# The loop over two iterations becomes one straight order of 80 attention jobs, and the first pair's last layers stand between the second pair's jobs

## The reference, cut to what matters

```python
# L0: modulated norm, self-attention with rotary embedding, gate, cross-attention, gate, MLP (gelu), gate
x = x + g_msa * self_out;  x = x + g_x * cross;  x = x + g_mlp * mlp_out
# L1: cross-attention on a normalised context
x = x_q + (out @ Wp + bp)
# L2: self-attention, gate, cross-attention, MLP (gelu), gate
x = x + h * gate_msa;  x = x + h;  x = x + h * gate_mlp
# L3: one-head attention on the context, a router over 3 experts (silu), a sigmoid gate
weights = softmax(scores);  routed = sum_e expert_out_e * router_probs_e
x = x + g * (routed @ out_w + out_b)
```

## Time and profile before

| | |
|---|---|
| time before, median of 3 runs | 987.18 us (987.16 to 987.22) |
| the profiled execution's own time | 980.62 us |
| its span | 978.7 us |
| PE busy | 780.3 us (80%) |
| DVE, ACT, POOL busy | 468.3, 325.2, 203.1 us |
| mean granted TensorE clock | 0.856 of full speed |

### The profile page before, as it was taken

How to read it: one execution, slowest core, us unless ns; L and a number is a source line. 1 busy time by engine, 2 the same in 40 slices (tenths; PEclk the granted TensorE clock), 3 DMA queues, 4 the chain that set the end, 5 groups by cost and what they waited for, 6 DMA issues and landing times.

```text
span 978.7 us, 22436 instructions
## 1 busy us (share of the span) xinstructions
PE 780.3 (80%) x9226; PEld 474.7 (49%) x9226; DVE 468.3 (48%) x1111; ACT 325.2 (33%) x544; POOL 203.1 (21%) x239
## 2 busy tenths in 40 slices
PE   5688888787788788868947888878878878887797
PEld 4244444545454455554633445454544445555447
DVE  3557544444455755332146566545344676343403
ACT  0123334233323333325421233352423233224362
POOL 1323221212123322010013233213022223111000
PEclk9799978858778987689979999996777899659899
DMA  8300000000000000000031000000000000000000
GB/s 299 109 1 13 13 1 2 2 1 2 2 2 2 2 2 2 1 0 1 1 109 50 2 3 1 2 1 1 2 1 2 1 2 2 1 2 1 1 0 23
DMA packets 5360, 16.26 MB, mean 17 GB/s; under 512 B 1577, under 2 KB 2612, under 8 KB 4360
## 3 DMA queue, kind: packets, MB, share of 16 engines
q1 hardware_dynamic: 4588, 10.72, 3.3%
q10 hardware_dynamic: 668, 4.05, 1.1%
HBM read 13.66 MB, written 1.09 MB: 15 GB/s over the span
## 4 chain that ended last, share of the span: by engine, by line
PE 65%; ACT 13%; DVE 11%; issue 8%; POOL 1%; DMA 1%; DVEq 0%; SPq 0%; ACTq 0%; POOLq 0%
PE avp L1006 15%; PE lin L889 12%; PE big L981 11%; PE lin L902 10%; ACT P L528 7%; ACT hT L515 4%; PE big L957 3%; DVE mhl L734 2%; PE big L989 2%; PE lin L911 2%; PE big L977 2%; DVE hid L758 2%; PE mtp L963 2%; PE big L974 1%; DVE xn L696 1%
## 5 line engine op out<-in xcount | busy, mean ns | idle before, releaser
L528 ACT ACTIVATE P<-big 77x1024 f32<-77x1024 f32 (+1 forms) x160 | 154.6, 1017 | 406.0 <-PE big L989 406.0
L734 DVE TENSOR_REDUCE mhl<-big 128x8 bf16<-128x616 f32 (+1 forms) x160 | 152.8, 964 | 108.2 <-PE big L957 105.3
L889 PE MATMUL lin<-hT,W 128*128 128x512 f32 x184 | 115.4, 734 | 39.5 <-ACT hT L515 37.0
L469 POOL TENSOR_TENSOR qm<-qT,hm 128x512 f32<-128x512 f32 x80 | 88.6, 1108 | 198.6 <-PE big L989 104.3
L981 PE MATMUL big<-qm,kT 32*77 32x512 f32 (+1 forms) x640 | 111.1, 770 | 0.0
L1006 PE MATMUL avp<-P,Vp 77*32 77x128 f32 (+1 forms) x2560 | 99.7, 304 | 4.0 <-ACT P L528 4.0
L1006 PE MATMUL avp<-P,onesp 77*32 77x128 f32 (+1 forms) x2560 | 101.4, 308 | 0.0
L436 POOL TENSOR_SCALAR rstd<-mv 128x4 f32<-128x4 f32 (+1 forms) x36 | 8.3, 230 | 433.0 <-DVE mv L687 432.8
L957 PE MATMUL big<-kbm,qb 32*128 32x308 bf16 (+1 forms) x320 | 57.4, 359 | 50.4 <-ACT P L528 50.2
L1006 PEld LDWEIGHTS avp<-P,Vp 77*32 77x32 f32 (+1 forms) x2560 | 73.8, 120 | 29.9 <-issue 19.4
L1006 PEld LDWEIGHTS avp<-P,onesp 77*32 77x32 f32 (+1 forms) x2560 | 85.7, 126 | 1.2
(11 more groups left out here) (153 smaller groups left out, 843.2 us busy)
## 6 DMA issues: line engine op xcount, KB each, us to landing
gbc<-gate_rows SPq DMA_DIRECT2D x4, 1280.0 KB, 8.8
W<-in_w ACTq DMA_DIRECT2D x2, 1152.0 KB, 12.3
hid<-in_ws SPq DMA_DIRECT2D x2, 832.0 KB, 5.7
W<-in_w ACTq DMA_DIRECT2D x1, 1088.0 KB, 6.7
xin<-in_x SPq DMA_DIRECT2D x4, 256.0 KB, 4.8
out<-x SPq DMA_DIRECT2D x4, 256.0 KB, 2.2
ctx<-in_ctx SPq DMA_DIRECT2D x4, 154.0 KB
ctxT<-in_ctxT SPq DMA_DIRECT2D x4, 154.0 KB
```

Of the source, the lines that this page charges most:

```text
L469: nc.gpsimd.tensor_tensor(qm[:, j % 2], q.broadcast_to([128, 4, T]), mask.broadcast_to([128, 4, T]), ALU.mult).then_inc(qm_ready, 1)
L528: nc.scalar.activation(P[j % 2][0:kw, 8 * half:8 * half + 8, :], big[0:kw, 2 * half:2 * half + 2, :].rearrange("p g (h q) -> p (g h) q", h=4),
L734: v.tensor_reduce(mhl[:].rearrange("p (g c) -> p g c", c=32)[:, 2 * half:2 * half + 2, 0:4], big[:, 2 * half:2 * half + 2, 0:4 * kw].rearr ...
L889: i = mm(lin_ap(st, s, job, m)[:, 0:n], w, a, start=(c == 0), stop=(c == len(parts) - 1))
```

## The change

The loop goes. All 16 samples are held at once: `NS` is 4 groups, and `ORDER` lists 20 blocks of four jobs: groups 0 and 1 through all five attentions, then groups 2 and 3. There are 80 jobs in one list. Each group has seven chains of units (`CHAINS`), one ahead of each attention and one behind the last, and each unit has a share of the way from the chain's first slot to its last; a slot is a quarter of a job. For the last chain `TAILS` gives the slots: group 0's from job 36 to the start of job 51, group 1's from job 40 to the start of job 56; groups 2 and 3 run over the end.

So that this fits, `x` is loaded once into `xs` for all groups; the gates come one at a time through a ring of four (`gring`) in place of 1,280 KB for each group and iteration; `Vp` and `hid` are shared by groups 0 and 2 and by 1 and 3; there is one `P`; the rope and the gated sums use `oT` for their partial result. Norm semaphores are one per group. The waits are on constants.

```diff
-NS = 2
-ITERS = B // (GB * NS)
+NS = B // GB
...
-for _k in range(NAT):
-    UNITS += merge(_k, 0, BETWEEN[_k], 1) + merge(_k, 1, BETWEEN[_k + 1], 0)
-UNITS += [("END", None, None)] + weave([("B", u, 0) for u in LAST],
-                                       [("B", u, 1) for u in [u for _, u in BETWEEN[NAT]] + LAST])
+ORDER = [(k, 2 * pair + s) for pair in range(2) for k in range(NAT) for s in range(2)]
...
+TAILS = [(16 * 9, 16 * 12 + 12), (16 * 10, 16 * 14), (16 * 19, END + 60), (END, END + 60)]
...
+def chain_slots(k, s):
+
+    if k == NAT:
+        return TAILS[s]
+    end = 16 * POS[k, s] - 6
+    if k:
+        return 16 * (POS[k - 1, s] + 1), end
+    return max(16 * POS[k, s] - 28, 0), end
...
+            for share, u in chain:
+                slot = first + round(share * (last - first))
...
+for _slot in range(END):
+    UNITS.append(("A", _slot // 4, _slot % 4))
+    UNITS += [("B", u, s) for slot, u, s in PLACED if slot == _slot]
+UNITS += [("END", None, None)] + [("B", u, s) for slot, u, s in PLACED if slot >= END]
...
-        P = [sb(f"P{i}", [128, H, T]) for i in range(2)]
+        P = sb("P", [128, H, T])
...
+        Vp2 = [sb(f"Vp{i}", [128, GB, H, 32]) for i in range(2)]
+        hid2 = [sb(f"hid{i}", [128, 7, N]) for i in range(2)]
...
+            def values(a, s):
                 st, kw = f"p{a}", ATT[a]["kw"]
-                lin_ready(dve, it, st, s, "v")
+                earlier = [p for (_, s2), p in POS.items() if s2 % 2 == s % 2 and p < POS[a, s]]
+                if earlier:
+                    dve.wait_ge(av_full, job_turn(max(earlier) * GB + GB - 1))
+                lin_ready(dve, st, s, "v")
...
-            with pe.Fori(0, ITERS) as it:
-                for kind, u, s in UNITS:
+            for kind, u, s in UNITS:
```

More of the change, by code:

```diff
@@ L110 @@
[L110 to L121, removed]
-]
@@ L124 @@
[L124 to L131, removed]
-    out = []
[L134 to L137, removed]
@@ new lines, with values_slot, placed @@
+TAILS = [(16 * 9, 16 * 12 + 12), (16 * 10, 16 * 14), (16 * 19, END + 60), (END, END + 60)]
[6 more added lines that the diff above has]
+    return max(16 * POS[k, s] - 28, 0), end
+def values_slot(k, s):
+    p = POS[k, s]
+    before = [q for (_, s2), q in POS.items() if s2 % 2 == s % 2 and q < p]
+    return 16 * (max(before) + 1) if before else 0
+def placed():
+    out = []
+    for s in range(NS):
+        for k, chain in enumerate(CHAINS):
+            if (k, s) == (0, 0):
+                continue
+            first, last = chain_slots(k, s)
+            for share, u in chain:
+                slot = first + round(share * (last - first))
+                if u == (f"p{k}", "v"):
+                    slot = max(slot, values_slot(k, s))
+                    assert slot < 16 * POS[k, s] + 3
+                out.append((slot, u, s))
+    return sorted(out, key=lambda e: e[0])
@@ L164 @@
             _n += 1
-LIN_JOBS = _n
-assert LIN_JOBS % 2 == 0
 def lin_bank(st, s, job):
     return LIN_AT[(st, s, job)] % 2
[L173 to L181, removed]
@@ L183, with lin_turn @@
-GATED = ["o0", "o1", "m0", "o3", "m1", "x3"]
[L184 to L197, removed]
-def job_of(j):
-    return j // (NS * GB), j // GB % NS, j % GB
-def nth(it, k, s, kinds, b=0, per=1):
-    return it * (kinds * NS * per) + (k * NS + s) * per + b + 1
+def lin_turn(st, s, job):
+    return LIN_AT[(st, s, job)] // 2 + 1
@@ new lines, in order_of, with groups_of @@
+def order_of(s, *wanted):
+    return [u[0] for kind, u, s2 in UNITS if kind == "B" and s2 == s and u in wanted]
+def groups_of(unit):
+    return [s for kind, u, s in UNITS if kind == "B" and u == unit]
+GATED = ["o0", "o1", "m0", "o3", "m1", "x3"]
+LN_ORDER = [[int(st[1:]) for st in order_of(s, *((f"l{k}", "stat") for k in range(NLN)))] for s in range(NS)]
+GATED_ORDER = [order_of(s, *((st, "y") for st in GATED)) for s in range(NS)]
+GATE_USES = [(u[0], s) for kind, u, s in UNITS if kind == "B" and u[1] == "y" and u[0] in GATED and u[0] != "x3"]
@@ new lines, with norm_turn, gated_turn, job_turn @@
+QB_ORDER = [(int(u[0][1:]), s) for kind, u, s in UNITS if kind == "B" and u[0][0] == "p" and u[1] == "q"]
+NGB = 4
+assert all(groups_of(("x3", part)) == groups_of(("x3", "s")) for part in X3_PARTS)
+assert all(groups_of(("p0", part)) == list(range(NS)) for part in "kq")
+def norm_turn(k, s):
+    return LN_ORDER[s].index(k) + 1
+def gated_turn(st, s):
+    return GATED_ORDER[s].index(st) + 1
+def job_turn(j, part=0, per=1):
+    return j * per + part + 1
+def job_of(j):
+    return ORDER[j // GB] + (j % GB,)
@@ new lines, in _ @@
+            sp.wait_ge(gate_rows_out, 16)
+            for n in range(NGB):
+                gates(n)
+            used = 0
+            for kind, u, s in UNITS:
+                if kind == "B" and u[1] == "y" and u[0] in GATED:
+                    sp.wait_ge(x_ready[s], gated_turn(u[0], s))
+                    if u[0] == "x3":
+                        sp.dma_start(out[:, s * GB:(s + 1) * GB, :], xs[s][:]).then_inc(stored[s], 16)
+                    else:
+                        used += 1
+                        if used + NGB <= len(GATE_USES):
+                            gates(used + NGB - 1)
@@ L423, in _ @@
+            for s in range(NS):
+                sp.wait_ge(stored[s], 16)
         @block.gpsimd
@@ new lines, in _ @@
+            for kind, u, s in UNITS:
+                if kind == "START":
+                    act.wait_ge(gate_rows_out, 16)
+                elif kind == "A" and s == 0:
+                    exps(u, 0)
+                    exps(u, 1)
+                elif kind == "B":
+                    st, part = u
+                    k = int(st[1:])
+                    if part == "t":
+                        norm(k, s)
+                    elif st[0] == "p":
+                        project(k, s, part)
+                    elif st[0] == "m" and part != "y":
+                        mlp(k, s, int(part[1:]))
+                    elif st == "x3":
+                        mixture(s, part)
```

625 lines of the change are left out of this document (292 added, 333 removed), and 6 rows, old and new, of the table CHAINS.

## The result

The changed kernel takes **941.86 us** (median of 4 runs, 940.23 to 946.37), the kernel before took 987.20 beside it (987.16 to 996.67). The ratio is 0.9525, 95% interval 0.9459 to 0.9592. I had forecast 910 with a range of 885 to 945: the direction and the range held, and the size was off by 32 us, 45 us saved where 77 were forecast.

A forecast was written before the change was run, and what follows sets the result against it. PE was taken to bound the kernel, busy 780.3 of 978.7 us, with waits and a lowered clock. Terms −122.9 + 85 − 14 − 9 + 5 − 1 − 12 − 6 − 3 = −78 took 987.2 to 909, stated as 910, range 885 to 945.

The forecast's parts named there:

- The gap: Between the two iterations' attention jobs, 404.1 to 527.0 us: this stretch goes, −122.9 us.
- its PE work: PE work from the stretch between the iterations comes back between attention jobs: +85 us, +93 if nothing runs faster.
- the filled waits: In the 20 jobs receiving the moved work, units fill idle PE time: −14 us, bounds 0 and −29.
- the clock there: In the 20 jobs receiving the moved work, PE falls less to its lower clock: −9 us, between 0 and −14.
- the loads: On ACT, 18 more function table loads, 23.1 us, mostly hidden: +5 us, bounds 0 and +23.1.
- Rival B: ACT binds the mixed jobs, so all table loads show and the filling is lost: 942 us, chance 0.17.
- case A: The likeliest case, PE-bound filling as the terms sum: 885 to 932 us, chance 0.62.
- Rival C: The PE clock comes back everywhere, wider spacing lifting 0.83 and 0.77 to 0.93: 876 us, chance 0.15.
- Chains are spaced wider: In the chains, wider spacing of producers and consumers cuts PE's waits for `hT` and `xn`: −12 us, bounds 0 and −30.
- clock from fewer long waits: In the stretches at clock 0.83 and 0.77, fewer long waits make it fall less often: −6 us, bounds 0 and −79.
- Head (−1) and last tail (−3): Group 1's norm and keys leave the start, −1 us; `l7` and half of `m1`'s group 2 matmuls precede the end, −3.
- At nothing: Single `P`, the gate ring's loads and the wait for `av_full` ahead of `v` were each taken to cost nothing.

The follow-up runs named there:

- the one chain mended: The changed kernel with the whole chain between attentions 1 and 2 put back at the old kernel's quarters: 910.5 us, and 907.11 us when repeated.
- The block kernel: The changed kernel with the last layers of the first pair in one block at job 40 instead of between the second pair's jobs: 979.64 us.
- all chains set back: The changed kernel with all four chains between attentions at the old kernel's quarters, last layers and head still spread: 939.71 us.

## Why the forecast was right in direction and too large

*The gap, its PE work, the filled waits, the clock there, the loads (−56 together).* Right. The stretch saved 45.5 us as it was and 52.7 with the one chain mended (298.4 to 245.7), at the forecast clock of 0.95 to 0.96. The block kernel shows that 31 of the 45.5 us of the stretch are the laying between jobs. The terms give 223 us of busy PE and 20 of idle there; measured were 227.4 and 25.4, and with the chain mended 224.5 and 21.2. The load term of +5 was measured at about +6. The mark of 240 us was missed by 6 with the chain mended, by 13 without.

*Rival B, ACT binds the mixed jobs.* Not what happened. In the changed kernel PE's waits for `P` in that stretch are some 4 us, not over 30:

```profile
PE big L1001 <- DVE mT L751: 7.5, 4, 2.8
PE lin L923 <- DVE xn L702: 3.8, 1, 3.8
PE big L962 <- ACT P L546: 3.0, 5, 1.1
```

The time, 942, is where B had put it, by another cause. That it lies within the range is luck in part: case A alone ended at 932, and the range went to 945 for B's sake. The Trainium skill's rule (ScalarE: Activation LUTs, "Table sets: the hidden batching unit") would have the loads gathered; the run without them says that here this could bring at most some 8 us. Nor is the 2.66 us per switch of the Trainium skill (the same page, "What ACT_TABLE_LOAD costs") seen: 1.31 us lie between the end of the exponentials and the start of the gelu in job 13 (163.45 and 164.76), and the stretch fell by 7.9 us without 25 loads, where 25 times 2.66 would be 67.

*Rival C.* Not seen: the clock outside the mixed jobs was 0.77 to 0.82 in jobs 12 to 36 and 56 to 79, as before. Its price was also summed wrongly: lifting 0.83 and 0.77 to 0.93 gives back 239.8 × 0.10 + 166.8 × 0.16 = 51 of the 79 us, not half, and C's time would have been 865 instead of 876.

*Chains are spaced wider (−12) and clock from fewer long waits (−6).* **This is the step that failed.** It treated the new slots as wider everywhere and named l3, l5 and l6 as like job 6. Two large parts of opposite sign stood in it. The chains ahead of attentions 1, 3 and 4 are wider, and this is worth about −29 to −33 us, more than my term (all chains set back against chain 2 alone set back). The chain ahead of attention 2 was laid worse, norm 2 at 0, 2 and 2 for 0, 4 and 5, and this costs 32 to 36 us (942.8 against 910.5 and 907.1). Of these, 13 go with one slot of the transposes and 11 with the chain's second half; the gelus behind the exponentials, which I had named, could not be priced apart. I had read the order at job 6 and carried it over, instead of working out each chain's slots, where two shares that round to one number would have been seen. A further price was the clock, which I had set beside the waits as a small term: in jobs 12 to 20 PE waited some 12 us in two places for `xn`, and the stretch became 14.8 us longer than with the chain mended, 5 of it longer PE busy time (80.20 against 75.25) for the same matmuls.

*Head (−1) and last tail (−3).* Measured −1.3 and −5.9, from one profile of each kernel.

*At nothing (one `P`, the ring, `av_full`).* PE, DVE, ACT and POOL have no wait for the ring in the changed kernel, and DVE's waits ahead of `Vp` are for the projection, not for `av`. One `P` was not tried against two.

*What would show it.* PE's share of 82% and 41 loads came as stated; its busy time was 767.9 for 765 or less, and 753.2 in the mended kernel. "Wrong if the stretches before and after got longer than 327.6 and 207.3" was the mark to look at: the first (jobs 0 to 36) took 339.0 instead of 327.7. The second, to the end of job 79's `av`, took 211.7 in this profile and 205.4 in the next, which decides nothing.

**Open** stays why jobs 20 to 36 with before's order ran at 0.76 in the changed kernel and at 0.82 in the kernel before, with nearly the same waits. The head of group 2 begins in job 33 now, and 6.2 of the 14.0 us lie in jobs 34 and 35, where PE waits 1.6 us longer. But 4.4 us lie in jobs 30 and 31, where PE waits as long as before (4.3 and 4.2 us) and the clock is 0.72 instead of 1.00, and job 24 took 10.6 us for 9.1. So it isn't shown either by which wait the spread chains gain their 30 us: the waits changed little, the clock did.

## What to carry to other kernels

When positions come from rounded shares of a span, print the slots for each chain and look at each pair of producer and consumer: with 10 slots a tenth is one quarter, and two steps in one quarter made PE wait 3.8 to 6.9 us, four times. Where such a wait is long, put matmuls that are ready (`av`) ahead of the transpose (13 us here); where it was 2 us or less, this gained nothing. Don't move the apply ahead of DVE work that PE waits for sooner: the waits of 2 us that this removed came back as waits of 3.1 to 4.1. And a forecast of "spaced wider" needs a sum for each chain, since a net near zero can hide two parts of 30 us.
